# A graph layer whose degree one-hots and second duplicate search read one input from PSUM

## The reference

```python
def gcn_conv(x, src, dst, w, W, b, n):
    xw = x @ W
    deg = jax.ops.segment_sum(w, dst, num_segments=n)
    dinv = jnp.where(deg > 0, jax.lax.rsqrt(deg), 0.0)
    norm = dinv[src] * w * dinv[dst]
    return jax.ops.segment_sum(xw[src] * norm[:, None], dst, num_segments=n) + b

h = layernorm(x); h = relu(gcn_conv(h, ..., W1, b1)); h = gcn_conv(h, ..., W2, b2)
x = x + relu(batchnorm(h) * gamma + beta + layernorm(x))
x = x + moe_top2(layernorm(x))          # 8 experts, each 256 -> 512 -> 256 with gelu
```

## Time and profile before

| | us |
|---|---|
| median of three runs | 2427.58 |
| lowest and highest | 2427.42, 2430.82 |
| the profiled execution | 2432.78 |
| its span | 2431.0 |
| POOL busy | 1699.6 |
| PE busy | 1910.6 |
| DVE busy | 898.5 |

### The profile page before, as it was taken

How to read it: one execution, slowest core, us unless ns; L and a number is a source line. 1 busy time by engine, 2 the same in 40 slices (tenths; PEclk the granted TensorE clock), 3 DMA queues, 4 the chain that set the end, 5 groups by cost and what they waited for, 6 DMA issues and landing times.

```text
span 2431.0 us, 29957 instructions
## 1 busy us (share of the span) xinstructions
PE 1910.6 (79%) x8514; PEld 1353.7 (56%) x8515; DVE 898.5 (37%) x2676; ACT 426.4 (18%) x1140; POOL 1699.6 (70%) x1679
## 2 busy tenths in 40 slices
PE   1184306899999997777999999999973737999998
PEld 0172204565555555554555656555543727999997
DVE  7993200222222224333223233333237773333332
ACT  0801000000000001110000000000004663444443
POOL 1887777777777777765777777777767444666675
PEclk6556757999999999898999999999985558999999
DMA  9997103656565654445555555656562145888885
GB/s 318 340 325 231 31 0 115 197 184 208 182 209 182 195 171 120 135 120 182 174 184 188 182 191 175 194 173 191 170 211 97 61 142 136 211 213 206 212 211 127
DMA packets 264105, 431.16 MB, mean 177 GB/s; under 512 B 39376, under 2 KB 147599, under 8 KB 263855
## 3 DMA queue, kind: packets, MB, share of 16 engines
q1 hardware_dynamic: 181167, 253.79, 31.3%
q0 software_dynamic: 81088, 173.80, 27.4%
q10 hardware_dynamic: 1728, 2.13, 0.3%
HBM read 339.36 MB, written 91.16 MB: 177 GB/s over the span
## 4 chain that ended last, share of the span: by engine, by line
POOL 55%; issue 18%; PE 16%; DVE 6%; DMA 3%; ACT 1%; SPq 0%; POOLq 0%; DVEq 0%; ACTq 0%
POOL arena L572 44%; POOL pair_weights L557 10%; PE psum L1680 7%; PE psum L1688 7%; DMA out_dram<-ACC 1%; PE psum L1671 1%; DVE edge_cols L1213 1%; DVE stats L1219 1%; DVE X L1216 1%; PE psum L1466 1%; DMA rows_for_experts<-ACC 1%; PE psum L1629 0%; DVE ACC L1322 0%; DVE ACC L1208 0%; DMA arena<-conv_rows,edge_cols 0%
## 5 line engine op out<-in xcount | busy, mean ns | idle before, releaser
L572 POOL DMA_INDIRECT arena<-conv_rows,edge_cols x1120 | 1066.9, 953 | 366.1 <-issue 366.1
L1507 PE MATMUL psum<-arena,X 128*128 128x512 f32 x1568 | 745.9, 600 | 46.8 <-DMA arena<-pair_weights 32.8
L1555 PE MATMUL psum<-arena 128*128 128x256 f32 x2240 | 599.1, 394 | 230.1 <-DMA arena<-conv_rows,edge_cols 220.1
L1555 PEld LDWEIGHTS psum<-arena 128*128 128x128 f32 x2240 | 423.5, 196 | 460.0 <-issue 363.8
L1507 PEld LDWEIGHTS psum<-arena,X 128*128 128x128 f32 x1568 | 299.7, 192 | 264.9 <-issue 212.3
L1143 DVE TENSOR_TENSOR ACC<-ACC,psum 128x256 f32 x80 | 33.7, 422 | 980.7 <-PE psum L1525 980.2
L557 POOL DMA_INDIRECT pair_weights<-scale_b,mean_b x224 | 252.2, 1126 | 117.1 <-issue 67.9
L1119 DVE TENSOR_SCALAR arena<-iota,edge_cols 128x128 f32<-128x128 f32 x1120 | 296.9, 362 | 6.1 <-issue 6.0
L647 POOL DMA_INDIRECT out_dram<-ACC x105 | 166.3, 1584 | 108.6 <-DMA out_dram<-ACC 77.3
L726 ACT ACTIVATE arena<-psum 128x256 f32<-128x256 f32 x80 | 30.7, 384 | 1045.2 <-PE psum L1555 1045.0
L1680 PE MATMUL psum<-ACC,arena 128*128 128x128 f32 x1680 | 207.9, 277 | 0.2 <-DVE ACC L1355 0.2
(11 more groups left out here) (287 smaller groups left out, 1432.2 us busy)
## 6 DMA issues: line engine op xcount, KB each, us to landing
arena<-pair_weights SPq DMA_DIRECT2D x371, 256.0 KB, 4.6
arena<-in_L_ffn_W_dram SPq DMA_DIRECT2D x113, 512.0 KB, 7.9
pair_weights<-zeros SPq DMA_DIRECT2D x4, 12544.0 KB, 65.1
arena<-conv_rows,edge_cols POOLq DMA_INDIRECT x1120, 2.8
conv_rows<-X SPq DMA_DIRECT2D x14, 896.0 KB, 5.8
X<-in_x_dram SPq DMA_DIRECT2D x12, 896.0 KB, 11.4
rows_for_experts<-ACC SPq DMA_DIRECT2D x7, 910.0 KB, 4.3
arena<-pair_weights SPq DMA_DIRECT2D x3, 1792.0 KB, 17.4
```

Of the source, the lines that this page charges most:

```text
L572: pool.indirect_dma_start(G[:, n * D:(n + 1) * D], None, y_tab[layer], bass.IndirectOffsetOnAxis(srcT[:, t:t + 1], 0)).then_inc(gathered[n ...
L1507: ins = m.matmul(bank(6 + c, BW), X[:, t * D + c * P:t * D + (c + 1) * P], table, start=(t == 0), stop=(t == NT - 1))
L1555: ins = m.matmul(bank(2 * (k % 2), D), S[:, n * P:(n + 1) * P], G[:, n * D:(n + 1) * D], start=(j == 0), stop=(j == GT - 1))
```

## The change

Nothing of the arithmetic is changed. In the second half of the duplicate search, and in the one-hots, one of an instruction's two tensor inputs is read from a copy in PSUM instead of SBUF. The copies are made by three instructions that are added at the start of the second half: of the keys (bank 7), of the weights (bank 3) and of the row 0 to 127 (bank 7). The bf16 `iota_b` and POOL's instruction that made it are gone; the one-hots read the 128 numbers in PSUM, each 14 times by a step of zero. `lo_b` (bf16) becomes `lo_f` (float32), made by the same instruction. The one-hots are still written to SBUF in bf16.

```diff
-        iota_b = early(GT * P, BF16)
-        lo_b, second = early(EC, BF16), early(EC, BF16)
+        lo_f, second = early(EC), early(EC, BF16)
...
+        key_p, iota_p, w_p = bank(7, RH), bank(7, RH + P)[:, RH:RH + P], bank(3, RH)
...
-                g.iota(iota_b.rearrange("p (n t) -> p n t", t=GT), [[1, P], [0, GT]], base=0, channel_multiplier=0,
-                       allow_small_or_imprecise_dtypes=True)
...
                 for h in range(2):
+                    key0, wrow0 = (key_p[0:DR, :], w_p[0:DR, :]) if h else (key, wrow)
+                    if h:
+                        v.tensor_copy(key0, key)
+                        v.tensor_copy(iota_p, iota[:, 0:P])
+                        chain(v.tensor_copy(wrow0[:, HALO:RH], wrow[:, HALO:RH]))
                     for c in range(MAXIN // 8):
-                        chain(v.tensor_tensor(same, key[:, o:o + SPAN].unsqueeze(1).broadcast_to([DR, 8, SPAN]),
+                        chain(v.tensor_tensor(same, key0[:, o:o + SPAN].unsqueeze(1).broadcast_to([DR, 8, SPAN]),
                                               sliding(key, o + d0, 8, 1, SPAN), ALU.is_equal))
-                        v.tensor_tensor(wsame, same[:, :, HALO:SPAN], sliding(wrow, o + HALO + d0, 8, 1, HW), ALU.mult)
+                        v.tensor_tensor(wsame, same[:, :, HALO:SPAN], sliding(wrow0, o + HALO + d0, 8, 1, HW), ALU.mult)
...
-                v.tensor_copy(lo_b, dst_lo[:, :].bitcast(I32))
+                v.tensor_copy(lo_f, dst_lo[:, :].bitcast(I32))
...
                                 v.tensor_tensor(lob[:, q * GT * P:(q + 1) * GT * P].rearrange("p (n t) -> p n t", t=GT),
-                                                iota_b.rearrange("p (n t) -> p n t", t=GT),
-                                                lo_b[:, bass.ds(i * (2 * DQ * GT) + q * GT, GT)].unsqueeze(1).broadcast_to(
+                                                iota_p.unsqueeze(2).broadcast_to([P, P, GT]),
+                                                lo_f[:, bass.ds(i * (2 * DQ * GT) + q * GT, GT)].unsqueeze(1).broadcast_to(
                                                     [P, P, GT]), ALU.is_equal).then_inc(lob_ready, 1)
```

## The result

The changed kernel takes **2402.19 us** (median of 4 runs, 2401.73 to 2402.92); the kernel before, beside it, 2427.50 (4 runs, 2427.03 to 2430.82). The ratio is 0.9894, interval 0.9880 to 0.9908: 25.3 us less, well over the 4.9 us that can be told from nothing. The forecast was 2404, with a range of 2398 to 2419.

What follows compares the result with a forecast made beforehand. POOL's queue was taken as the bound, the first gather waiting for 224 scatters. Gains of 20.9 us beside the one-hots and 2.6 in the duplicate search, 23.5 together, took 2427.6 to 2404 us, range 2398 to 2419.

Steps and rivals of the forecast that it cites:

- The bound: POOL's queue: the first gather starts only when 224 scatters have been issued, so shorter scatters move all that follows.
- The price on DVE: One-hots going from bf16 to float32: 2025 ns instead of 1079 each, 53 us more DVE work for 56.
- The copies: Three copies into PSUM on DVE: about 1 us, hidden because eight scatters, 10 us, are still to be issued.
- The release: Scatters beside the one-hots: 91 lose 0.02 us each, 1.6 us left of 22.5, a gain of 20.9 us.
- The duplicate search: Scatters beside the search's second half: 2.6 of 3.9 us lost regained, as the eight short instructions per pass stay unreleased.
- The sum: 20.9 + 2.6 = 23.5 us earlier for the first gather and all behind it, giving 2404 us.
- The cover: DVE's work ahead of the gathered rows ends at 329 us, rows arrive at 359: 30 us left, longer DVE costs nothing.
- The wait of PE: PE's wait before the first gathered rows: to shrink from 116 to about 30 us.
- The hold: Long two-input operations at the one-hots keep POOL out even with PSUM: 45 us lost, 2450 us, chance 0.08.
- half of it: One-hots with one SBUF input still cost each scatter 0.2 us: gain only 9.3 us, 2418 us, chance 0.11.
- The small copies: DVE's 56 unchanged copies beside the one-hots cause the scatters' loss: only 2.6 us go, 2425 us, chance 0.04.
- The rival of a late DVE: One-hots needing two passes (3.9 us) end DVE 158 us later, delaying PE: 51 us longer, 2479 us, chance 0.04.

Runs made afterwards that it cites:

- two reductions: Changed kernel plus two unused reductions reading PSUM ahead of each one-hot, some 70 us more DVE work: 2408.01 us, ratio 0.9921.
- the one-hots alone: Changed kernel with the duplicate search put back on SBUF, so only the one-hots read PSUM: 2402.39 us, ratio 0.9896.
- that part alone: Kernel before, with only the second half of the duplicate search reading PSUM and its one-hots unchanged: 2423.25 us, ratio 0.9981.
- the run with float32 in SBUF: Changed kernel, but the one-hots read the same float32 numbers from SBUF instead of PSUM: 2441.74 us, ratio 1.0057.
- the run with one reduction: Changed kernel plus one unused reduction reading PSUM ahead of each one-hot, some 35 us more DVE work: 2399.70 us, ratio 0.9887.

## Why the prediction was right, and where its sizes were off

- **The bound.** "The first gather starts when 224 scatters have been issued, and at nothing else": it held in every kernel (the first gather follows at the usual 0.30 us). First gathers from 343.87 to 397.39 us went with times from 2393.84 to 2441.74, to some microseconds, except where two reductions made DVE late.
- **The price on DVE.** 2025 ns forecast for a one-hot from three rows of other lines, 2017 measured; 53 us forecast, 52.5 measured. The copies took 57.36 to 58.45, 1.1 us, as forecast and hidden. (The 0.07 us that the prediction gave each of them as its fixed part stands on no row: the line through the earlier trace rows gives 684 - 512 x 1.048 = 147 ns.)
- **The release.** The prediction took 0.02 us as the loss of each of 91 scatters; measured is none in 93. (Its product was a slip: 91 x 0.02 is 1.8, not 1.6, so its sum should have been 23.3.) At the one-hots 20.9 us were forecast and 34 x 0.662 = 22.5 came, all of what was lost; the one-hots alone moved the first gather by 21.7, and most of the other 0.8 is that their first scatter started 0.6 us later (58.71 instead of 58.11).
- **The duplicate search.** 2.6 us forecast; what is left of 3.9 is 23 x (993 - 960) = 0.8, so 3.1 came (3.95 for that part alone). I had guessed that the released scatters would meet the eight short instructions more often. They hardly do: by their starts, 10 of 20 stood beside a short one before and 11 of 23 after, and these lose at most 0.24 us (1.20 instead of 0.96).
- **The sum.** 23.5 us forecast at the first gather, 26.4 measured; both sizes that were off, were off to the cautious side. The two parts make 22.5 + 3.1 = 25.6; 0.7 more came between the search and the split, where the change touches only the output type of one cast. From 87.2 to 95.2 us five scatters of 1306 ns on average lost 1.7 us before, and from 88 to 96 us six of 1131 ns lost 1.0 after. The scatters came at other moments there and met other instructions: luck, not forecast. The time fell by 25.3.
- **The cover.** "Ends at 329, no later": it ended at 322.2, since the wait for the early tables shrank from 32.8 to 25.3 us, which the prediction had left out as a possible help. Gathered rows were forecast for 359 and came at 356.34, so the cover left was 34 us, not 30. The wait of PE, forecast at 30, was 42: I had taken it from the end of DVE's matrices, but the trace counts it from PE's last transpose, 8 us earlier.
- **The rivals.** The hold's price was right to a microsecond, but for a one-hot that reads SBUF (45 us, the run with float32 in SBUF); with PSUM there is no hold and no half of it. The small copies fell with the same run. The prediction cited the Trainium skill ("SBUF — State Buffer", Who interferes with whom) for them with copies alone as those that take both sides; the section names casts and tensor-scalar operations as well, and its sentence on two SBUF inputs, which the prediction left out, speaks for the forecast. The rival of a late DVE had the right place and point (it begins to bite at 84 us of delay by the prediction; PE's last transpose was 81 us later than before, 347.5 instead of 266.3, in the run with one reduction, which cost nothing, and 113 later in the one that cost 5.8 us), but a wrong price: I had set PE's delay equal to the time's. POOL's lead of two groups and PE's faster pace absorb most of it.

## What to carry to other kernels

Where POOL issues DMAs on the path that sets the end, look at the pitch of its issues beside DVE's long two-input instructions: if it falls into step with them, give one of their inputs a copy in PSUM, or cut them short, which here got two thirds of the gain, at a turn close to the scatter's own pitch. The copy in PSUM can pay even if it doubles DVE's time, as long as DVE has cover; work out that cover from the wait of the engine behind it. And read a part worth a few microseconds from the place that it moves (here the first gather), since the time behind it varies by more: here by nine microseconds from kernel to kernel.

## What the runs showed that I had not expected

- Instructions of 448 elements with both inputs in SBUF cost a scatter only 0.06 us, in step with a turn of 1.31 us; those of 1792 float32 elements cost it 0.77 us, in step with a turn of 2.03.
- The stretch behind the first gather, in which all kernels do the same work, took 2043.5 to 2052.4 us in the eight profiled executions without a wait of POOL for PE. The gathers take 1427.4 to 1431.8 us of it, from the first to the last, and the part behind them 615.6 to 620.6; what sets either stays open.
- DVE writes 352, 128 and 304 float32 elements into PSUM in 0.52, 0.28 and 0.47 us.
- The split's instructions of 784 elements take 8.00/3 = 2.67 us of DVE each, with an input in PSUM as with both in SBUF, longer than the one-hots of 1792 elements at 2.02; their output is scattered in steps of six elements, and whether that is the reason was not tried.
- One SBUF input is not always free. In the kernel before, between the search and the split, a scatter beside two casts of one SBUF input takes 1.28 us, 0.32 more than 0.96, as if held until the first of them is through:

```profile
88.55 0.62 DVE L959 CAST ACC<-arena 128x896 bf16<-128x896 int32 x1
89.08 0.62 DVE L960 CAST arena<-arena 128x896 f32<-128x896 int32 x1
...
88.72 1.28 POOL L557 DMA_INDIRECT pair_weights<-scale_b,mean_b  x1 [0.30 <-issue]
```

L1040, also with one tensor input in SBUF, costs 0.03 us. What the casts have that L1040 lacks was not tried; so the runs show that PSUM frees these two-input operations, and not that one SBUF input is free whatever the operation.
